# Eight passes of a two-layer recurrent network in one unrolled program, without barriers between the passes

## What is computed

```
x1  = x + softmax_attention(x_normed) * silu(moe(x_normed))     # 16 heads of 8, causal; 8 experts, top 2
out1 = delta_rule(layernorm(x1))                                # 4 heads of 32, chunks of 32 tokens, EMA mix
y   = local_attention_network(layernorm(x1), depth 2)           # 8 heads of 64, window 64, gated MLP
out = x1 + silu(y) * (rmsnorm(out1) @ Wo)
```

## Time and profile before

| | |
|---|---|
| median of 3 runs | 2782.47 us |
| lowest and highest | 2780.78 and 2790.22 us |
| profiled execution, its own time | 2787.48 us |
| span in the profile (first to last instruction) | 2785.7 us |
| PE busy | 2044.7 us (73% of the span), 20756 matmuls |
| ACT, DVE, POOL busy | 50%, 49%, 19% of the span |
| mean granted clock of PE | 0.847 of full speed |

### The profile page before, as it was taken

The page is one execution under the profiler, slowest core; times in us unless marked ns, Lnnn a source line. Parts: engine busy times, 40 slices in busy tenths (PEclk is TensorE's granted clock), DMA queues, the critical chain, the costliest instruction groups (busy, mean ns, idle before and its releaser), DMA issues. The chain is left out here.

```text
span 2785.7 us, 52043 instructions
## 1 busy us (share of the span) xinstructions
PE 2044.7 (73%) x20756; PEld 1155.9 (41%) x20756; DVE 1361.2 (49%) x3156; ACT 1401.0 (50%) x3612; POOL 540.6 (19%) x609
## 2 busy tenths in 40 slices
PE   1405574679867987798778896898679877987767
PEld 0203233344543455344534463455344543445334
DVE  2502324554546553745464646555555546553542
ACT  0311351377437752766267634774386537662433
POOL 0360200302022201311040304020312022210220
PEclk9957685789879987998889987998789879987788
DMA  5362200200020002000020002000200020000000
GB/s 185 107 165 71 69 2 12 47 2 2 13 52 2 2 9 57 1 2 5 14 47 3 1 14 51 2 1 13 52 2 2 13 52 1 2 7 12 1 1 4
DMA packets 97257, 76.32 MB, mean 27 GB/s; under 512 B 44451, under 2 KB 87804, under 8 KB 94814
## 3 DMA queue, kind: packets, MB, share of 16 engines
q1 hardware_dynamic: 92894, 66.35, 9.4%
q0 software_dynamic: 4096, 6.32, 1.3%
HBM read 41.55 MB, written 33.16 MB: 27 GB/s over the span
## 5 line engine op out<-in xcount | busy, mean ns | idle before, releaser
L1128 ACT ACTIVATE work_a<-PS,work_a 128x512 bf16<-128x512 f32 (+3 forms) x512 | 263.3, 530 | 77.2 <-DVE work_a L1244 75.4
L1986 POOL TENSOR_TENSOR work_b<-work_b,tables 128x256 f32<-128x256 f32 x256 | 209.3, 837 | 376.1 <-DVE work_b L1870 376.1
L1775 ACT ACTIVATE work_b<-PS,neg_max 128x192 f32<-128x192 f32 (+1 forms) x512 | 201.2, 417 | 125.0 <-DVE neg_max L1910 76.0
L1244 DVE TENSOR_REDUCE work_a<-PS 128x2 f32<-128x1024 f32 (+3 forms) x256 | 200.3, 820 | 104.0 <-PE PS L882 102.0
L1145 ACT ACTIVATE work_a<-PS 128x1024 f32<-128x1024 f32 (+1 forms) x192 | 169.9, 885 | 107.6 <-PE PS L912 106.4
L1550 PE MATMUL PS<-wqkv,hT 128*128 128x512 f32 x384 | 198.0, 646 | 8.7 <-DVE work_b L1870 6.4
L1585 PE MATMUL PS<-k,q 64*128 64x192 f32 (+1 forms) x1024 | 146.9, 419 | 55.6 <-ACT shiftT L1761 35.1
L930 PE MATMUL PS<-work_a 128*64 128x512 f32 (+3 forms) x1024 | 182.6, 459 | 0.0
L2000 POOL TENSOR_TENSOR rstd_b<-var_eps_b,minus_half 128x4 f32<-128x4 f32 x16 | 16.4, 1025 | 787.2 <-DVE var_eps_b L121 787.2
L1791 ACT ACTIVATE work_b<-PS 128x768 f32<-128x768 f32 (+1 forms) x128 | 97.1, 759 | 106.8 <-PE PS L1628 106.8
L1585 PEld LDWEIGHTS PS<-k,q 64*128 64x128 f32 x1024 | 98.8, 243 | 96.3 <-ACT shiftT L1761 40.5
(11 more groups left out here) (297 smaller groups left out, 4222.5 us busy)
## 6 DMA issues: line engine op xcount, KB each, us to landing
work_a<-stack_d SPq DMA_DIRECT2D x32, 512.0 KB, 10.1
stack_d<-parts SPq DMA_DIRECT2D x48, 192.0 KB, 3.8
stack_d<-parts SPq DMA_DIRECT2D x32, 128.0 KB, 2.7
x_all<-in_L_attn_x_dram SPq DMA_DIRECT2D x4, 512.0 KB
slots_in<-xn_all SPq DMA_DIRECT2D x1, 2048.0 KB, 9.4
xnT_d<-xnT_all SPq DMA_DIRECT2D x1, 2048.0 KB
xn_all<-slots_in SPq DMA_DIRECT2D x8, 256.0 KB, 3.4
slots_out<-xn_all SPq DMA_DIRECT2D x8, 256.0 KB, 2.2
```

Of the source, the lines that this page charges most:

```text
L1128: nc.scalar.activation(dump0[:, n % 2 * T:n % 2 * T + (i + 1) * P], PS[:, a:a + (i + 1) * P], ACT.Exp, bias=neg_max0[:, k:k + 1], accum_ou ...
L1244: nc.vector.reduce_max(neg_max0[:, 2 * g * NT + i:(2 * g + 2) * NT:NT], at[:, :, Q_AT[i]:Q_AT[i] + (i + 1) * P], AX_X, negate=True).then_i ...
L1775: nc.scalar.activation(dump2[:, n % 4 * 256:n % 4 * 256 + w], PS[:, a:a + w], ACT.Exp, bias=neg_max2[:, k:k + 1], accum_out=sums2[:, k:k + ...
L1986: nc.gpsimd.tensor_tensor(to[:, n, :, r, :], src[:, n, :, 1 - r, :], table(2 * n + 1, t)[:, 32 * r:32 * r + 32].unsqueeze(1).to_broadcast( ...
```

## The change

All passes become one block of one program. The loop, the block ends and the barriers between the passes go, and with them the resetting of the semaphores; each wait now counts on from batch to batch (`ofa`, `ofd`, `past` and `once` add the increments of the batches done). `x1`, `y` and `out1` exist twice, and the streams take the set of the batch's parity, so stream A writes straight into the buffers that stream B reads, and the copies L2078, L2079 and L2094 go. The shifted copies to `hT` and the clearing of its corner move to stream B's first slice. Where the barrier kept the areas apart, waits take its place: PE, POOL and SP wait for `mixed` (the last DVE instruction of the delta rule) before they start the next batch's attention, ACT waits for it before the square, and the first copy into `v2` waits for the output store of the batch before. Batch numbers are constants. The order of the slices on each engine is kept: the 17 slices that stood at the end of a pass stand ahead of stream B's first slice of the next.

```diff
-        x1_a = sb("x1_a", T)
-        xn_a = sb("xn_a", T)
+        x1s = [sb(f"x1_{n}", T) for n in range(2)]
+        ys = [sb(f"y_{n}", T) for n in range(2)]
+        out1s = [sb(f"out1_{n}", T) for n in range(2)]
...
+        def counted(table, done):
+            return lambda name, n=0: done * table[name] + n
...
         def attention_pe(pe, b):
-            pe.wait_ge(sa["xT"], 16)
+            ofa, ofd = counted(A_COUNTS, b), counted(D_COUNTS, b)
+            if b:
+                pe.wait_ge(sd["mixed"], ofd("mixed"))
+            pe.wait_ge(sa["xT"], ofa("xT", 16))
...
         def attention_pool(gp, b):
-            nc.gpsimd.tensor_copy(from_b[:, :], slot_from[:, bass.ds(b * 2 * NT, 2 * NT)]).then_inc(sa["from_b"], 1)
...
+            if b:
+                gp.wait_ge(sd["mixed"], ofd("mixed"))
+            nc.gpsimd.tensor_copy(from_b[:, :], slot_from[:, b * 2 * NT:(b + 1) * 2 * NT]).then_inc(sa["from_b"], 1)
...
         def attention_sp(sp, b):
-            sp.dma_start(xnT_b[:, :], xnT_d[bass.ds(b * P, P), :]).then_inc(sa["xT"], 16)
+            if b:
+                sp.wait_ge(sd["mixed"], ofd("mixed"))
+            sp.dma_start(xnT_b[:, :], xnT_d[b * P:(b + 1) * P, :]).then_inc(sa["xT"], 16)
...
         def local_pe(pe, b, l):
...
+                    if t == 0 and l == 0:
+                        pe.wait_ge(s["hT_rows"], once("hT_rows", 1))
+                        pe.wait_ge(s["hT_zero"], once("hT_zero", 1))
...
         def local_act(act, b, l):
             if l == 0:
+                if b:
+                    act.wait_ge(s["hidden"], past("hidden"))
+                act.wait_ge(sd["T_copied"], D_COUNTS["T_copied"] * (b + 1))
+                nc.scalar.copy(hT[0:64, :], xnT_a[0:64, :])
+                nc.scalar.copy(hT[64:P, 1:T], xnT_a[64:P, 0:T - 1]).then_inc(s["hT_rows"], 1)
                 nc.scalar.preload_act_table_set(LN_EXP)
+                act.wait_ge(sd["mixed"], D_COUNTS["mixed"] * (b + 1))
                 nc.scalar.square(hs[:, :], out1[:, :]).then_inc(s["o_sq"], 1)
...
+                    if b and l == 0 and t == 0:
+                        act.wait_ge(s["stored"], 16 * b)
                     nc.scalar.copy(v2[:, t * 512:(t + 1) * 512], bank(6)).then_inc(s["v_copied"], 1)
...
         def local_dve(dve, b, l):
             if l == 0:
-                dve.wait_ge(s["o_inverse"], 1)
+                if b:
+                    dve.wait_ge(s["hidden"], past("hidden"))
+                nc.vector.memset(hT[64:P, 0:1], 0.0).then_inc(s["hT_zero"], 1)
+                dve.wait_ge(s["o_inverse"], once("o_inverse", 1))
...
         def local_sp(sp, b):
-            sp.wait_ge(sb_["final"], 1)
-            sp.dma_start(out[bass.ds(b, 1)].rearrange("o (t p) f -> p (o t) f", p=P),
+            sp.wait_ge(sb_["final"], b + 1)
+            sp.dma_start(out[b:b + 1].rearrange("o (t p) f -> p (o t) f", p=P),
                          final.rearrange("p (t f) -> p t f", f=P)).then_inc(sb_["stored"], 16)
-            sp.wait_ge(sb_["stored"], 16)
+            if b == B - 1:
+                sp.wait_ge(sb_["stored"], 16 * B)
...
-        A_AHEAD = (0, 0, 2, 1, 0, 0, 0, 0, 0, 4, 2, 0, 1, 0, 2, 0, 0, 0, 2, 2, 2, 1, 2, 2, 1, 1, 2, 2, 1, 3, 1, 0, 1, 1,
+        A_LEAD = 76
+        A_AHEAD = (17, 0, 2, 1, 0, 0, 0, 0, 0, 4, 2, 0, 1, 0, 2, 0, 0, 0, 2, 2, 2, 1, 2, 2, 1, 1, 2, 2, 1, 3, 1, 0, 1, 1,
                    2, 1, 1, 2, 1, 2, 1, 1, 1, 4, 2, 0, 1, 1, 1, 1, 5, 1, 1, 4, 0, 1, 0, 0, 2, 0, 0, 0, 1, 1, 0, 1, 1, 0)
...
+        ORDER = ["A"] * A_LEAD
+        for b in range(B):
             for ahead in A_AHEAD:
-                woven_order += ["A"] * ahead + ["B"]
-            return woven_order + ["A"] * (A_SLICES + D_SLICES - sum(A_AHEAD))
+                ORDER += ["A"] * min(ahead, B * (A_SLICES + D_SLICES) - ORDER.count("A")) + ["B"]
...
-        run(0, None)
-        with nc.Fori(0, B - 1) as b:
-            run(b + 1, b)
-        run(None, B - 1)
+        with nc.Block() as block:
+            @block.tensor
+            def _(pe):
+                woven(ORDER, {"A": stream_a(attention_pe, delta_pe, pe), "B": stream_b(local_pe, pe)})
...
+        end_phase()
```

More of the change, by code:

```diff
@@ L1498, in delta_sp, with local_pe @@
                 yield
[L1501 to L1505 removed]
+        def local_pe(pe, b, l):
+            s, past, once = sb_, counted(PER_LAYER, b * DEPTH + l), counted(PER_BATCH, b)
+            y, out1 = ys[b % 2], out1s[b % 2]
             if l == 0:
[L1508 removed]
+                pe.wait_ge(s["o_sq"], once("o_sq", 1))
                 nc.tensor.matmul(bank(7), cst[:, C_BLK32:C_BLK32 + P], hs[:, :], start=True, stop=True
@@ L2018, in layers @@
-        def layers(local, handle):
-            for l in range(DEPTH):
-                yield from local(handle, l)
-        A_AHEAD = (0, 0, 2, 1, 0, 0, 0, 0, 0, 4, 2, 0, 1, 0, 2, 0, 0, 0, 2, 2, 2, 1, 2, 2, 1, 1, 2, 2, 1, 3, 1, 0, 1, 1,
-                   2, 1, 1, 2, 1, 2, 1, 1, 1, 4, 2, 0, 1, 1, 1, 1, 5, 1, 1, 4, 0, 1, 0, 0, 2, 0, 0, 0, 1, 1, 0, 1, 1, 0)
-        if len(A_AHEAD) != DEPTH * B_SLICES or sum(A_AHEAD) > A_SLICES + D_SLICES:
-            raise ValueError("one count per slice of stream B")
@@ L2106, in network, with stream_a, stream_b, stream_b_sp @@
-        run(0, None)
-        with nc.Fori(0, B - 1) as b:
-            run(b + 1, b)
-        run(None, B - 1)
+        def stream_a(attention, delta, handle):
+            for b in range(B):
+                yield from attention(handle, b)
+                yield from delta(handle, b)
+        def stream_b(local, handle):
+            for b in range(B):
+                for l in range(DEPTH):
+                    yield from local(handle, b, l)
+        def stream_b_sp(handle):
+            for b in range(B):
+                yield from local_sp(handle, b)
@@ new lines, in network @@
+        A_LEAD = 76
+        A_AHEAD = (17, 0, 2, 1, 0, 0, 0, 0, 0, 4, 2, 0, 1, 0, 2, 0, 0, 0, 2, 2, 2, 1, 2, 2, 1, 1, 2, 2, 1, 3, 1, 0, 1, 1,
+                   2, 1, 1, 2, 1, 2, 1, 1, 1, 4, 2, 0, 1, 1, 1, 1, 5, 1, 1, 4, 0, 1, 0, 0, 2, 0, 0, 0, 1, 1, 0, 1, 1, 0)
+        if len(A_AHEAD) != DEPTH * B_SLICES or sum(A_AHEAD) != A_SLICES + D_SLICES or A_LEAD + A_AHEAD[0] < A_SLICES + D_SLICES:
+            raise ValueError("one count per slice of stream B, and all slices of stream A")
+        ORDER = ["A"] * A_LEAD
```

441 lines of the change are left out of this document (197 added, 244 removed).

## The result

| | before | after |
|---|---|---|
| median (lowest to highest, runs) | 2786.34 us (2780.78 to 2801.43, 4) | 2760.43 us (2751.05 to 2764.62, 4) |
| profiled execution, its own time | 2787.48 us | 2759.51 us |

The ratio is 0.9894 with the interval 0.9846 to 0.9942: 26 us or 1.1% faster, where 2733 us (2717 to 2751) was forecast. The direction was right, and about half of the gain is missing. Between the profiled executions the gain is 28.0 us.

The account below looks back on a forecast made before the run. PE counts inside passes; its 79.5 us of waits at eight seams was the target. From the profiled 2787.48 us, less 50.1 for seams, plus 1.0 for POOL: 2738.4; 5.0 lower on the median's scale, 2733 us, range 2717 to 2751.

Parts of the forecast that it names:

- The seams: Between the nine passes: PE's idle time at eight seams falls from 79.5 to 29.4 us, giving 50.1 us.
- The floor of 3.67 us per seam: PE's remaining idle time per seam: 2.94 us to L1387's end, two hand-offs of 0.05, the square of 0.63.
- The hand-off that could not be seen: At the seam, from DVE's end of the delta rule to ACT's square: assumed 0.05 us.
- ACT's late restart: At the seam, ACT starts 2.83 us after POOL; read as late code after the jump back, gone without it.
- The rival that it stays: Code supply does not improve: six seams keep 17 us, gain 33 us, total 2750 us; chance 0.10.
- The table load: ACT's 1.28 us load, once per batch, moves ahead of the wait for `mixed` into idle time, so hidden.
- POOL's tie: After the seam, POOL's slack before L1986 shrinks from 4.2 to 0.1 us; loss of 1.0 us in seven passes.
- my two bounds: POOL's lateness per pass with a gather: between 0 and 0.3 us, 0.15 taken.
- The loads: At a pass's start, the `xnT` load and the stack's large loads lose their lead but cause no wait.
- I take the stretches as unchanged: Between the seams: stretches keep their length, mean 282.1 us, since slice order is kept; only seams are priced.
- My sum keeps the mean: Clock drops can be worth up to 7.9 us a pass between seams; the sum uses the mean stretch regardless.
- the clock falls badly: Rival: all seven stretches as the slowest, +26 us, 2759; chance 0.10 for moving over about 15 us, both sides.

Follow-up runs that it names:

- e1_unrolled_barriers: Kernel before with only the hardware loop written out as seven passes; barriers, copies and single buffers kept: 2779.45 us, ratio 0.9953.
- the delay: Three idle ACT squares before the real one per seam: 2765.14 us against the changed kernel's 2756.13; with one bias matmul, 2728.58 against 2727.94.

## Why the prediction was wrong, and where it was right

- **The seams.** 50.1 us were forecast, 50.3 measured. The floor of 3.67 us per seam is 29.2 / 8 = 3.65. The hand-off that could not be seen, from DVE to ACT, took 0.04 us where I gave 0.05.
- **ACT's late restart was the jump.** The part of which I was least sure held: the square follows L1410 at once, and `e1_unrolled_barriers` gave 21.4 us for the jump alone. The rival that it stays would have shown waits of 6.5 us at the six seams, and the longest is 3.7. The median of 2760 is near its 2750 only by accident.
- **The table load is hidden.** It stands 16 us ahead of the square. No row shows a cost, nor a drain ahead of the square.
- **POOL's tie.** POOL is now late by a third of a microsecond: its last gather ends at 2273.48 and its next work starts then, while DVE's L1908 had ended at 2273.17.

```profile
2272.48 1.00 POOL L1426 DMA_INDIRECT work_a<-slots_out,work_a  x1 [0.30 <-issue]
2272.49 0.68 DVE L1908 TENSOR_TENSOR work_b<-PS,inv 128x512 f32<-128x512 f32 x1
2273.50 1.66 POOL L2021 TENSOR_TENSOR work_b<-work_b,tables 128x256 f32<-128x256 f32 x2
```

That is the upper of my two bounds, 0.3, not the 0.15 taken: at most 2.3 us instead of 1.0. I can't show that it reaches PE, since the first 83 us of a stretch last as long as before (83.6 against 83.9 us in the mean).
- **The loads.** No wait for them at L862 or L892, as forecast. Nothing shows an engine waiting for its code inside the passes: the six parts that vary little differ by 0.3 us in all, and 162 + 72 instruction packets were fetched where it had been 179 + 88.
- **The step that failed** is "I take the stretches as unchanged", and with it "My sum keeps the mean". I had the row that warned: stretches of equal work from 277.91 to 285.81 us. I priced the whole spread at a chance of 0.10, with the argument that the seven of before were spread over both ends. In the changed kernel the mean moved by 3.0 us a stretch, in its two repeats it stood 2.9 and 2.0 us above the 282.1 of before's repeat (the second of them on another chip). Of the 49.1 us forecast between the profiled executions 28.0 came, and the 20.7 us of the stretches are the difference but for 0.4. The rival "the clock falls badly" had the right mechanism; its chance was far too low, its ends took no account of a stretch of 289.1 us, and my range cut it off at 16 us.
- **The base.** Three runs of 2780.78 to 2790.22 us showed before as steadier than it is. Its runs on three other chips go from 2765.11 to 2823.65 us, so part of any difference of 10 us between two sets of four runs is chance. Against before on the same chip the change gives 26, 40 and 34 us (2786.34 - 2760.43, 2806.64 - 2766.84, 2790.36 - 2756.13), by the ratios 30, 38 and 30. None reaches 50.

**What is shown and what is open.** Shown: the gain of the seams is whole, the loss lies in the stretches, it goes with PE's clock and not with waits, and it comes mostly from three parts. In one of them the fall depends on when the part begins against the clock's grid, in both kernels alike. Open: why the unrolled kernels meet the falls more often, and what decides in the other two parts, which hold 2.1 of the 3.0 us. My explanation is that the loop's restarts vary (seams of 10.3 to 11.4 us), so the passes begin at varied points against the grid, while equal seams of 3.89 us repeat a bad point from pass to pass. For it speak the ranges above. Against it speaks that `e1_unrolled_barriers`, with equal seams too, lost only 4 to 8 us by its runs, and that the delay seemed to help where the suspect part had no falls. It is argued, not shown. Seven stretches a profile are too few to tell a habit from chance: after had the fall 4, 3 and 1 times of 7, before 2 and 0. That one bias matmul removes the fall rests on the seven stretches named above. Open too: two stretches of after took 23.2 us in the part of the recurrence's start at clock 1.00, 1.2 us more than others of that clock, with no wait that names a cause.

**The best version** is the changed kernel with one bias matmul, at 0.9772 (0.973 to 0.9813) and the same in its other measurement, where the change alone gives 0.9892.

## What to carry to other kernels

A seam between passes can be priced from its timeline to a fraction of a microsecond: take the true chain of dependences and the hand-offs, and the rest of PE's wait is the gain. But where PE bounds the stretches and stretches of equal work differ in length, that spread times the number of passes belongs in the range of any change that shifts when the passes begin, however local the change is; a few executions of before show how wide it is. Look at the time of each stretch and of the profiled execution against its median before you read a mean of stretches: here it was up to 17 us off. And short matmuls that use one row are worth a look of their own: taking out three of four was worth 19 to 28 us here, against 26 to 40 for the whole restructuring, most of it for the work itself.

## What the runs showed of the hardware

- PE's clock fell from 2.4 to 1.2 GHz while PE was busy in 3.00 of 3.00 us, at one-row and 128x128 matmuls. Whether it fell differed between passes with the same instructions: 74.3 us, or 77.3 or 78.8. In 70 stretches of 70 it went with the time from a point of the clock's grid to the beginning of the part.
- With one one-row matmul of 512 columns in place of four of 128, none of the seven stretches that began the part where the others had fallen had the fall. The three matmuls fewer save 1.2 us (74.34 to 73.16 us).
- The jump back of the hardware loop costs 2.8 to 3.9 us a pass in this kernel (seams of 10.3 to 11.4 us, beside 7.50 without it); at the seam of the earlier trace rows, 10.7 us long, 2.83 of the 3.2 us are ACT's late restart. A barrier of all engines with the clearing of the semaphores, two copies of 0.4 us and the exposed table load of 1.28 us cost 3.6 us (7.50 - 3.89).
- Idle matmuls that filled 2.56 of 3 us ahead of the seam did not raise the clock clearly earlier: 3.3 to 3.7 us behind the first matmul of the pass, beside 3.3 to 4.4 us without them.
